# First attention of a two-layer decoder: query and key tiles hold every second pair of heads, and their parts go through DRAM in rows of 4 KB and 2 KB

## What is computed

```python
WQ, WK, WV, WO = (_quant_weight(w).T for w in (q_weight, k_weight, v_weight, o_weight))   # int4 steps per row
result, ch_bias, n = _chunk_decompose(hidden_states)     # 64-token chunks: bias removed, int4 steps per channel
...
q = (result + ch_bias) @ WQ + q_bias ; q *= 16 ** -0.5   # k and v alike, without the factor
scores = q @ k.T                                         # per batch and head: 256 x 256
attn = softmax(scores) @ v
x = layernorm(x + (quantized attn) @ WO + o_bias)
```

## Time and profile before

| | |
|---|---|
| median of 3 runs | 2344.27 us (2344.26 to 2346.66) |
| the profiled execution's own time | 2343.61 us |
| its span in the trace | 2341.8 us |
| first attention: prepare | 0 to about 99 us |
| first attention: core | about 99 to 470 us |
| PE, DVE, ACT, POOL busy over the span | 80%, 63%, 40%, 22% |
| DMA, share of the 16 engines' time | 31.6% on the queue of SP |

### The profile page before, as it was taken

How to read it: one execution, slowest core, us unless ns; L and a number is a source line. 1 busy time by engine, 2 the same in 40 slices (tenths; PEclk the granted TensorE clock), 3 DMA queues, 4 the chain that set the end, 5 groups by cost and what they waited for, 6 DMA issues and landing times. The chain is left out here.

```text
span 2341.8 us, 32975 instructions
## 1 busy us (share of the span) xinstructions
PE 1882.6 (80%) x12318; PEld 1404.6 (60%) x12318; DVE 1470.5 (63%) x2844; ACT 940.0 (40%) x1588; POOL 510.3 (22%) x500
## 2 busy tenths in 40 slices
PE   3248898856476999999999968999985998378886
PEld 2225555511344999999999957787863776134443
DVE  8846777545574566665666545657662776367776
ACT  1005556610232444444444423334434111377784
POOL 0032232024101010101010001001100887134442
PEclk9958999955688999999999988999997999689897
DMA  5089999221652212222222223222224113600100
GB/s 198 0 131 142 149 141 144 21 90 45 226 187 79 61 55 73 73 66 62 80 59 69 64 81 136 91 91 73 82 72 174 50 50 99 238 5 32 36 15 23
DMA packets 145837, 208.45 MB, mean 89 GB/s; under 512 B 13520, under 2 KB 84048, under 8 KB 143248
## 3 DMA queue, kind: packets, MB, share of 16 engines
q1 hardware_dynamic: 136720, 189.57, 31.6%
q10 hardware_dynamic: 8960, 16.78, 1.9%
HBM read 159.82 MB, written 46.22 MB: 88 GB/s over the span
## 5 line engine op out<-in xcount | busy, mean ns | idle before, releaser
L452 DVE TENSOR_REDUCE a_rowmax<-a_ring 128x2 f32<-128x512 f32 x256 | 165.1, 687 | 84.5 <-PE a_ring L534 82.5
L1557 DVE TENSOR_TENSOR f_hid<-f_gate,f_gu 128x256 f32<-128x256 f32 x264 | 108.4, 421 | 162.6 <-ACT f_gate L1429 160.0
L1429 ACT ACTIVATE f_gate<-f_gu 128x256 f32<-128x256 f32 x264 | 98.3, 381 | 274.2 <-PE f_gu L1295 187.4
L2394 PE MATMUL e_py<-e_kv,e_toep 128*128 128x320 f32 x640 | 175.5, 438 | 3.8 <-DVE e_kv L2418 3.8
L397 ACT ACTIVATE a_prob<-a_sT 128x1024 f32<-128x1024 f32 x128 | 130.6, 1026 | 77.7 <-PE a_sT L523 77.6
L2394 PEld LDWEIGHTS e_py<-e_kv,e_toep 128*128 128x128 f32 x640 | 123.5, 193 | 55.6 <-issue 6.2
L1308 PE MATMUL f_gu<-f_lowh,f_bg 128*128 128x256 f32 x704 | 141.3, 283 | 5.2 <-POOL f_lowl L1214 5.0
L1295 PE MATMUL f_gu<-f_xhi,f_wg 128*128 128x256 f32 x704 | 130.3, 283 | 0.0
L1295 PE MATMUL f_gu<-f_xhi,f_wu 128*128 128x256 f32 x704 | 129.1, 282 | 0.0
L1308 PEld LDWEIGHTS f_gu<-f_lowh,f_bg 128*128 128x128 f32 x704 | 115.8, 191 | 9.7 <-POOL f_lowl L1214 5.2
L1562 DVE TENSOR_TENSOR f_hl<-f_hid,f_hh 128x768 fp32r<-128x768 f32 (+2 forms) x90 | 84.5, 939 | 55.9 <-ACT f_hh L1475 54.8
(11 more groups left out here) (372 smaller groups left out, 4951.2 us busy)
## 6 DMA issues: line engine op xcount, KB each, us to landing
f_entry<-in_WdT SPq DMA_DIRECT2D x89, 256.0 KB, 2.8
d_staging<-in_w SPq DMA_DIRECT2D x16, 1024.0 KB, 5.7
a_qs<-parts SPq DMA_DIRECT2D x96, 128.0 KB, 6.3
a_ks<-parts SPq DMA_DIRECT2D x96, 128.0 KB, 7.1
parts<-a_hi SPq DMA_DIRECT2D x16, 512.0 KB, 8.7
parts<-a_lo SPq DMA_DIRECT2D x16, 512.0 KB, 9.2
e_toep<-lags SPq DMA_DIRECT2D x32, 256.0 KB
f_entry<-in_Bg SPq DMA_DIRECT2D x89, 64.0 KB, 1.8
```

What stands on the lines that cost most here:

```text
L452: dve.tensor_reduce(rowmax[:, s % 2, :, e * SLOTS + j], ring[n % RING][:, :].rearrange("p (q t) -> p q t", t=T), AX.X, ALU.max, negate=Tru ...
L1429: act.activation(gate[:, i % 2, :], gu[n % 3][:, 0, :], ACT.Silu).then_inc(s_["gate_ready"], 1)
L1557: dve.tensor_tensor(hid[:, j, :], gate[:, i % 2, :], gu[n % 3][:, 1, :], ALU.mult).then_inc(s_["hid_ready"], 1)
L2394: last = pe.matmul(py[n % RING][:, 0:DIAG * BS], toep[:, h % 3, (t - j) * P:(t - j + 1) * P], kv[:, h % 2, :, j, :], start=(j == 0), stop= ...
```

## The change

The pairing of channels and partitions is changed for q and k. Before, group `f` of a tile held channels `f*128` to `f*128+127` of the half, that is four neighbouring pairs of heads; a stack's pair `j` lay in group `j // 4`. Now group `f` holds every second pair of heads: partition block `j` (32 partitions) has pair `2j` in group 0 and pair `2j+1` in group 1. So the two groups of one partition belong to neighbouring places of a stack, and their 2 x 1 KB can be moved as one row of 2 KB. `parts` becomes a tensor of [128 partitions, q or k, 512 values], to which each partition of `hi` or `lo` writes one row of 4 KB.

To have q and k in this order, their weights are loaded in it: `load_paired` issues 8 DMAs of 128 KB into 32 partitions each, for q on the SP queue and for k on the ACT queue, in place of one DMA of 1 MB each on SP. The biases come by 8 DMAs of 128 single values on the ACT queue. In the product with the chunk biases each group of 128 columns is split in four of 32, for q and k. V is as it was.

```diff
+        def load_paired(queue, w):
+
+            src = io["w" + "qk"[w]].rearrange("(h j f e) i -> h j e f i", h=2, j=ROWS, e=BLOCK)
+            for h in range(2):
+                for j in range(ROWS):
+                    queue.dma_start(natural[j * BLOCK:(j + 1) * BLOCK, w, 2 * h:2 * h + 2, :], src[h, j]).then_inc(got_w[w], 16)
+
...
-                for w, name in enumerate("qkvo"):
-                    sp.dma_start(natural[:, w, :, :], io[f"w{name}"].rearrange("(k p) i -> p k i", p=P)
-                                 ).then_inc(got_w[w], 16)
+                load_paired(sp, 0)
+                for w, name in enumerate("vo"):
+                    sp.dma_start(natural[:, 2 + w, :, :], io[f"w{name}"].rearrange("(k p) i -> p k i", p=P)
+                                 ).then_inc(got_w[2 + w], 16)
...
                     for o in range(KT):
-                        for k in range(KT):
-                            last = pe.matmul(offs[w % 2][:, o * NC:(o + 1) * NC],
-                                             wide[:, w, k, o * P:(o + 1) * P], xbias[:, k * NC:(k + 1) * NC],
-                                             start=(k == 0), stop=(k == KT - 1))
+                        for j in range(ROWS if w < 2 else 1):
+                            rows = slice(j * BLOCK, (j + 1) * BLOCK) if w < 2 else slice(0, P)
+                            c = (o // 2 * 2 * ROWS + 2 * j + o % 2) * BLOCK if w < 2 else o * P
+                            for k in range(KT):
+                                last = pe.matmul(offs[w % 2][rows, o * NC:(o + 1) * NC],
+                                                 wide[:, w, k, c:c + rows.stop - rows.start], xbias[:, k * NC:(k + 1) * NC],
+                                                 start=(k == 0), stop=(k == KT - 1))
...
             @block.scalar
             def _(act):
+                load_paired(act, 1)
+                for j in range(ROWS):
+                    for f in range(2):
+                        rows = slice(j % 2 * 64 + f * BLOCK, j % 2 * 64 + (f + 1) * BLOCK)
+                        act.dma_start(beta[j * BLOCK:(j + 1) * BLOCK, 0:2, f::2], io["b0"][rows, 0:2, j // 2::2],
+                                      allow_slow_non_contiguous=True).then_inc(got_beta, 16)
...
-                        sp.dma_start(io["parts"][a % 2, 0].rearrange("w (k p) t -> p w k t", p=P),
-                                     hi[:, a % 2, :, :, :].bitcast(F32)).then_inc(hi_out[a % 2], 16)
+                        sp.dma_start(io["parts"][a % 2, 0], hi[:, a % 2, :, :, :].bitcast(F32).rearrange("p w f t -> p w (f t)")).then_inc(hi_out[a % 2], 16)
...
-                                sp.dma_start(qs[a // 2 % 2][rows, pairs, :].bitcast(F32),
-                                             io["parts"][a % 2, qp, 0].rearrange("(j e d) t -> e d j t", e=2, d=HD0)[e]
+                                sp.dma_start(qs[a // 2 % 2][rows, pairs, :].bitcast(F32).rearrange("d (j f) t -> d j (f t)", f=F2),
+                                             io["parts"][a % 2, qp, :, 0].rearrange("(j e d) c -> e d j c", e=2, d=HD0)[e]
                                              ).then_inc(stack_in[a % 4], 16)
...
-SCRATCH = {"parts": ([2, 2, 2, D // 2, T], F32)}
+SCRATCH = {"parts": ([2, 2, P, 2, D // 2 // P * T], F32)}
```

More of the change, by code:

```diff
@@ L142, in attention0_prepare @@
         got_w = [sem(f"a0_got_w{w}") for w in range(4)]
-        got_x, got_wide = sem("a0_got_x"), sem("a0_got_wide")
+        got_x, got_wide, got_beta = sem("a0_got_x"), sem("a0_got_wide"), sem("a0_got_beta")
         steps, wq_ready = sem("a0_steps"), sem("a0_wq_ready")
@@ L148, in attention0_prepare @@
         cb_done, cb_free = sem("a0_cb_done"), sem("a0_cb_free")
+        BLOCK = 2 * HD0
+        ROWS = P // BLOCK
+        def load_paired(queue, w):
[3 more added lines that the diff above has]
+                    queue.dma_start(natural[j * BLOCK:(j + 1) * BLOCK, w, 2 * h:2 * h + 2, :], src[h, j]).then_inc(got_w[w], 16)
         with nc.Block() as block:
@@ L158, in _ @@
                                  ).then_inc(got_wide, 16)
-                sp.dma_start(beta[:, :, :], io["b0"]).then_inc(got_wide, 16)
+                sp.dma_start(beta[:, 2, :], io["b0"][:, 2, :]).then_inc(got_wide, 16)
             @block.gpsimd
@@ L170, in _ @@
                 for w in range(4):
-                    dve.wait_ge(got_w[w], 16)
+                    dve.wait_ge(got_w[w], 16 * (2 * ROWS if w < 2 else 1))
                     ch.step(dve.tensor_reduce(big[:, w * KT:(w + 1) * KT], natural[:, w, :, :], AX.X, ALU.max,
@@ L190, in _ @@
                 dve.wait_ge(got_wide, 64)
+                dve.wait_ge(got_beta, 16 * 2 * ROWS)
                 for w in range(3):
@@ L330, in _ @@
                         sp.wait_ge(hi_done, 2 * a + 2)
-                        sp.dma_start(io["parts"][a % 2, 0].rearrange("w (k p) t -> p w k t", p=P),
-                                     hi[:, a % 2, :, :, :].bitcast(F32)).then_inc(hi_out[a % 2], 16)
+                        sp.dma_start(io["parts"][a % 2, 0], hi[:, a % 2, :, :, :].bitcast(F32).rearrange("p w f t -> p w (f t)")).then_inc(hi_out[a % 2], 16)
                         sp.wait_ge(lo_done, 2 * a + 2)
-                        sp.dma_start(io["parts"][a % 2, 1].rearrange("w (k p) t -> p w k t", p=P),
-                                     lo[:, a % 2, :, :, :].bitcast(F32)).then_inc(lo_out[a % 2], 16)
+                        sp.dma_start(io["parts"][a % 2, 1], lo[:, a % 2, :, :, :].bitcast(F32).rearrange("p w f t -> p w (f t)")).then_inc(lo_out[a % 2], 16)
                         if real(s):
@@ L343, in _ @@
                                 rows = slice(e * 64 + r * HD0, e * 64 + (r + 1) * HD0)
-                                sp.dma_start(qs[a // 2 % 2][rows, pairs, :].bitcast(F32),
-                                             io["parts"][a % 2, qp, 0].rearrange("(j e d) t -> e d j t", e=2, d=HD0)[e]
+                                sp.dma_start(qs[a // 2 % 2][rows, pairs, :].bitcast(F32).rearrange("d (j f) t -> d j (f t)", f=F2),
+                                             io["parts"][a % 2, qp, :, 0].rearrange("(j e d) c -> e d j c", e=2, d=HD0)[e]
                                              ).then_inc(stack_in[a % 4], 16)
-                                sp.dma_start(ks[a // 2 % 2][rows, pairs, :].bitcast(F32),
-                                             io["parts"][a % 2, kp, 1].rearrange("(j e d) t -> e d j t", e=2, d=HD0)[e]
+                                sp.dma_start(ks[a // 2 % 2][rows, pairs, :].bitcast(F32).rearrange("d (j f) t -> d j (f t)", f=F2),
+                                             io["parts"][a % 2, kp, :, 1].rearrange("(j e d) c -> e d j c", e=2, d=HD0)[e]
                                              ).then_inc(stack_in[a % 4], 16)
```

## The result

The changed kernel takes 2331.74 us (2329.91 to 2335.17, five runs) beside 2344.27 us for the kernel before (2341.35 to 2346.66, five runs) on the same chip. The medians lie 12.5 us apart. The ratio is 0.9955, with a 95% interval of 0.9941 to 0.9970, which is 10.5 us (7 to 14) of the 2344.27: a small gain, but clear of no change. The profiled execution took 2329.91 us. The forecast was no change, 2344.7 us, so it was wrong.

A forecast was written before the change was run, and what follows sets the result against it. SP's DMA queue was taken to pace the first attention, with PE close behind. Terms: 2343.6 + 5.5 (start) - 3.5 (writes) - 1.6 (stacks) = 2344.0, plus 0.7 to the median, 2344.7 us; range 2327 to 2353.

The forecast's parts named there:

- The bound: First attention's core: SP's queue sets the pace at 18.60 us a turn, stack DMAs at 115 GB/s; PE needs 17.05.
- C: Rival for the stack DMAs: row count limits them, 200 GB/s or more, time 2315 us; chance 0.10.
- The start: Loading q's and k's weights into 32 partitions at 230 GB/s delays DVE and the whole loop: +5.5 us.
- ACT's issues: 16 issues on ACT's queue before its table load end near 10 us; cost 0.
- The products with the chunk biases: 128 matmuls instead of 32, 0.13 us each, 17 us against 14, hidden before DVE asks; cost 0.
- D: Slower rival: products with the chunk biases come out from under DVE, 14 us late, 2359 us; chance 0.10.
- E: Slower rival: loads into 32 partitions get little more than 115 GB/s, DVE 15.6 us late, 2355 us; chance 0.08.
- Stacks in, 2 KB rows, still 16 partitions: Stack DMAs in the attention core: partitions limit, longer rows gain 0.1 us per turn, -1.6 us in all.
- the doubled burst: Stack DMAs: if rows are buffered, 2 KB rows carry another 16 KB per pair, 0.92 us per turn, -14.7 us.
- A: Likeliest case: stack DMAs stay at the partitions' rate, 2344.7 us, own range 2340 to 2349; chance 0.55.
- B: Rival for the stack DMAs: partitions limit but 2 KB rows double the bursts, 14.7 us gained, 2331.6 us; chance 0.17.
- Parts out, 4 KB rows: Writes of the parts at 412 GB/s, 0.22 us shorter each, all 16 in the chain: -3.5 us, bounds 0 to -5.1.

The follow-up runs named there:

- e2: Kernel before, 1 KB rows kept, with each stack DMA's 16 partitions in steps of four: 2300.98 us, ratio 0.9829.
- e7: Changed kernel with the stack DMAs reordered so that the half of the partitions changes with every DMA: 2312.8 us, ratio 0.9881.
- e8: Kernel before, 1 KB rows, with the stack DMAs reordered so that the half of the partitions changes with every DMA: 2306.9 us, ratio 0.9854.
- e4: Changed kernel with 8 unused columns per slot in the parts, so writes go in 1 KB rows while reads stay at 2 KB: 2337.45 us, ratio 0.9986.
- e5: Changed kernel, unchanged, profiled and timed once more: 2329.62 us, ratio 0.9960 to the kernel before.
- e1: Kernel before, unchanged, profiled once more as a control: 2340.18 us, ratio 0.9994.
- e12: Kernel before, unchanged, profiled again as a second control: 2343.36 us, ratio 1.0007.
- e6: Changed kernel with k's weight load on ACT's queue starting in the other half of the partitions: 2331.62 us, ratio 0.9955.
- e9: Changed kernel with k's eight weight loads behind q's on SP's queue, none on ACT's: 2328.94 us, ratio 0.9950.
- e10: Kernel before with both partitions in steps of four and the half changing at each stack DMA: 2303.32 us, ratio 0.9838.

## Why the prediction was wrong

**What was right.** The bound: the core of the first attention is paced by stack DMAs on SP's queue, whose rate is set mainly by the 16 partitions that each fills. e2 shows this directly, since 1 KB rows into spread partitions run at 199 GB/s instead of 116. The rival in which the row count limits (C) is out: it wanted 200 GB/s from this change, which gave 120. The start: 230 GB/s was taken for loads into 32 partitions and 231 measured (4 to 12 us), so the bound of 7.9 us by 200 GB/s was too far; +5.5 us was forecast, and +5.7 came (mean of first parts at 128.69 and 128.68 against 122.86, 123.10 and 123.01), within the forecast 12 to 15 us for DVE's first reduction. ACT's issues ended at 10.5 us, as said, and delayed nothing. The products with the chunk biases stayed hidden: 7.19 us for 128 matmuls, 0.056 us each where 0.13 was taken, done at about 62 us, and DVE asks for them at 95.84. The slower rivals D and E are out.

**The step that failed.** It is the term *Stacks in, 2 KB rows, still 16 partitions*, which was set at 1.6 us. The core of the two profiles of the changed kernel is 336.6 us on average (337.1 and 336.1) and that of the three of the kernel before 347.3 (348.0, 348.9 and 345.1), so it gave 10.7 us. The writes account for at most 16 x 0.31 = 5.0 of these. What is left for the reads is at least 5.7 us, 0.36 per stack, between the 0.1 taken and the 0.92 that the doubled burst would give. The first stack alone shows a like size, 15.34 - 14.90 = 0.44 us, which is 7.0 over 16. So the term was some 6 to 8 us and not 1.6. The turn, over the same profiles, fell from 18.51 to 17.89 us, 0.6 where A had 0.2 to 0.4 and B 1.1, and the stack rate is 120, at the edge of A and B. So a gain such as B described is there at about half its price. That B's 2331.6 us is nearly the measured 2331.74 is luck: its stack term was 14.7. The reason against it, that a buffer counts bytes and not rows, decided between ends that the trace left open, and it was argued, not measured. e7 and e8 measure what more changes of partitions bring, 0.29 us each with the small row and 0.44 with the large one. These don't close the account. The 0.15 us more per change would be 0.9 us over a stack's six, twice what the change showed. Why, and whether rows or bytes are buffered, no run shows.

**A term less sure than it looked.** *Parts out, 4 KB rows* was taken at 3.5 us, from 0.22 us a write and all 16 of them in the chain. The rate was near: 401 GB/s in the window, for the 412 taken. The first landing became shorter by 0.31 us, at most 5.0 in all. By e4, where 5.4 us of 9.6 reached the core, it would be 2.8; this is an estimate, which would leave 7.9 for the reads. No run measures the writes alone.

**What stays open.** By the profiles the start costs 5.7 us and the core gives back 10.7, so the change brings 5 us, to about 2339. It is the same where the attention ends: 465.3 us (mean of the changed kernel and e5) against 470.3 (of before, e1 and e12). The core differs by up to 4 us between profiles of one kernel (345.1 to 348.9 before), and with the same core code e6 has 332.9 and e9 336.0, so this is 5 us give or take two or three. The ratios show 0.45% in the first comparison and 0.40% in e5's, 10.5 and 9.4 us. The 4 to 6 us between are not explained. In part they may lie in that spread; in the profiled pair the difference lies behind the attention, in code that is the same in both. There the fourteen profiles scatter from 1862 to 1871 us, with no order by kernel: before 1871.0, 1869.2 and 1867.8, changed 1862.3 and 1867.5, and e9 with the changed core 1870.7. The traces narrow down where. From 300 to 1265 us behind the weight load the fourteen agree within 1.2 us, and the differences arise before and after. They go with TensorE's clock: behind that load it was granted only the lower of its two levels (1.2 GHz) for 377.5 us in all in the changed kernel's first profile, 376.6 in e8 (1864.8 us), 389.6 in the first of the kernel before, and 402.9 and 403.5 in e9 and e10 (1870.7 and 1871.2 us). Over all fourteen the correlation with the time is 0.83, at about 0.3 us for each us at the lower level. That would be 3 to 4 of the 8.7 us between the first two profiles. It is a correlation: whether the clock made the difference or followed it, and whether the change moves it other than by chance, was not shown, and the cause is not settled.

## What to carry to other kernels

When a DMA fills few partitions, its rate belongs to them: step the partitions (16 in steps of four gave 199 GB/s for 116) or, where the layout is fixed, let the half of the partitions change with every DMA (134 and 153 GB/s for 116 and 121). The second edit is only one of order; the first also needs the rows between filled and the contraction widened. They brought 1.2 to 1.8% of the whole kernel, while the longer rows brought 0.4%, net of the 5.7 us paid for them in the loads. And where two bounds of a term differ by a factor of nine and decide the sign of the sum, give the term the middle and the case between a chance, not the end for which there is a good argument.

## What was not expected of the hardware

- An issue on SP takes longer when the partitions are stepped: 0.60 us instead of 0.43. With 128 KB each, that is the next limit at 205 GB/s.
- A gain for each further change of the 16 destination partitions, 0.29 us with rows of 1 KB and 0.44 with rows of 2 KB, for DMAs of one queue (one profile of each).
- Two queues that load the same 32 partitions in step: the weight of q is in at 13.95 us, at 12.17 if the other queue starts in the other half, and at 9.98 with both on one queue, q first.
- Fp32 matmuls with 32 weight columns and 32 moving columns took 0.056 us each, against 0.43 with 128 weight columns, both at a granted clock of 1.00.
- A write from a padded source (1 KB rows with a gap) took 3.29 us to land, against 3.00 for rows of 1 KB without a gap in the kernel before, where their places in DRAM are others.
